# A recurrence kernel on one Trainium2 core: the loads of the next block are issued after another step of the chunk

## The reference, cut to what matters

```python
def step(carry, xs):
    W_in, W_out = carry
    q_t, k_t, v_t, lr_t = xs
    k_h = softmax(einsum('blhd,bDhd->blhD', k_t, W_in)) * lr_t[..., 1:]
    q_h = softmax(einsum('blhd,bDhd->blhD', q_t, W_in))
    qk = einsum('bqhD,bkhD->bhqk', q_h, k_h) * mask
    o_t = einsum('bqhD,bDhd->bqhd', q_h, W_out) + einsum('bhqk,bkhd->bqhd', qk, v_t)
    W_out = W_out + einsum('bnhD,bnhd->bDhd', k_h, v_t)
    for _ in range(2):
        g_out = -attn(W_in, k_t, v_t)
        g_in = -attn(W_out, v_t, k_t)
        W_in = W_in - lr_in * g_in
        W_out = W_out - lr_out * g_out
    return (W_in, W_out), o_t
```

## Time and profile before

| | us |
|---|---|
| median of 3 runs | 2461.43 |
| lowest and highest | 2460.49, 2465.33 |
| the profiled execution | 2457.74 |
| its span in the trace | 2456.0 |

### The profile page before, as it was taken

The page is one execution under the profiler, slowest core; times in us unless marked ns, Lnnn a source line. Parts: engine busy times, 40 slices in busy tenths (PEclk is TensorE's granted clock), DMA queues, the critical chain, the costliest instruction groups (busy, mean ns, idle before and its releaser), DMA issues.

```text
span 2456.0 us, 88067 instructions
## 1 busy us (share of the span) xinstructions
PE 2143.7 (87%) x32669; PEld 1375.5 (56%) x32669; DVE 1602.1 (65%) x3901; ACT 1558.3 (63%) x4121; POOL 1100.0 (45%) x1221
## 2 busy tenths in 40 slices
PE   7999996878888877885699999999999999999898
PEld 4455452555555555553366565665655756657566
DVE  6888885676776776773277474773746847557465
ACT  6788883676676676664365484564845748547474
POOL 1212223676776777776423344234433343233323
PEclk9999998898998898887799999999999999999999
DMA  6655557333334333411421312312123112220120
GB/s 199 179 154 161 175 152 186 69 67 82 77 68 88 79 69 75 87 32 37 134 69 44 91 22 76 78 45 74 38 76 77 45 52 60 74 72 11 33 52 18
DMA packets 387235, 201.37 MB, mean 82 GB/s; under 512 B 257376, under 2 KB 372704, under 8 KB 386800
## 3 DMA queue, kind: packets, MB, share of 16 engines
q1 hardware_dynamic: 386800, 195.65, 30.3%
HBM read 101.67 MB, written 69.27 MB: 70 GB/s over the span
## 4 chain that ended last, share of the span: by engine, by line
PE 44%; DVE 16%; issue 15%; ACT 14%; POOL 7%; SPq 2%; DMA 1%; ACTq 1%; DVEq 1%; POOLq 0%
PE psum L1050 11%; ACT arena L1569 8%; DVE arena L1861 6%; PE psum L1143 4%; PE psum L1102 3%; PE psum L906 3%; PE psum L1110 3%; PE psum L900 3%; ACT arena L1368 2%; POOL arena L1637 2%; PE psum L1216 2%; PE psum L893 2%; PE psum L914 2%; PE psum L1082 2%; PE psum L1179 2%
## 5 line engine op out<-in xcount | busy, mean ns | idle before, releaser
L1795 POOL TENSOR_TENSOR arena<-arena 128x400 f32<-128x400 f32 x256 | 218.3, 853 | 481.9 <-DVE arena L2223 481.9
L1368 ACT ACTIVATE arena<-psum,scan_sb 64x128 f32<-64x128 f32 x1152 | 307.7, 361 | 115.0 <-PE psum L974 107.0
L1569 ACT ACTIVATE arena<-psum,arena 128x100 f32<-128x100 f32 x1024 | 270.0, 367 | 6.4 <-DVE arena L2215 6.3
L1861 DVE SCALAR_TENSOR_TENSOR arena<-psum,taps_sb,arena 128x511 f32<-128x511 f32 (+2 forms) x288 | 212.5, 747 | 55.1 <-ACT arena L1268 48.4
L808 PE MATMUL psum<-arena,w_in_sb 128*128 128x512 f32 x512 | 230.1, 598 | 1.0 <-ACT arena L1261 1.0
L1611 POOL TENSOR_TENSOR arena<-arena 128x512 f32<-128x512 f32 x64 | 80.7, 1273 | 264.5 <-ACT arena L1294 264.5
L900 PE MATMUL psum<-arena 128*32 128x17 f32 x10240 | 127.3, 192 | 80.7 <-issue 60.0
L1940 DVE TENSOR_TENSOR arena<-psum,scan_sb 64x512 f32<-64x512 f32 x290 | 188.5, 673 | 3.3 <-PE psum L1006 2.9
L2215 DVE TENSOR_REDUCE arena<-psum 128x4 f32<-128x400 f32 x256 | 146.3, 573 | 58.5 <-PE psum L1166 48.1
L1561 ACT ACTIVATE arena<-psum 100x512 f32<-100x512 f32 x256 | 156.1, 610 | 42.8 <-PE psum L1179 36.6
L906 PE MATMUL psum<-arena,scan_sb 128*128 128x512 f32 (+1 forms) x328 | 172.3, 612 | 11.1 <-ACT psum L1413 4.5
(11 more groups left out here) (225 smaller groups left out, 4711.7 us busy)
## 6 DMA issues: line engine op xcount, KB each, us to landing
arena<-arena SPq DMA_DIRECT2D x144, 128.0 KB
arena<-x SPq DMA_DIRECT2D x32, 512.0 KB, 4.0
arena<-gates_d SPq DMA_DIRECT2D x112, 128.0 KB, 4.0
v_rows_d<-arena SPq DMA_DIRECT2D x64, 136.0 KB
k_rows_d<-arena SPq DMA_DIRECT2D x64, 136.0 KB
arena<-k_rows_d SPq DMA_DIRECT2D x128, 68.0 KB, 2.1
arena<-v_rows_d SPq DMA_DIRECT2D x128, 68.0 KB, 2.3
v_d<-arena SPq DMA_DIRECT2D x32, 256.0 KB, 4.5
```

The costliest lines, as they stand in the source:

```text
L1368: ins = act.activation(dst.rearrange("p (t x a) -> p t x a", x=PP, a=INNER)[upper, :, x], src.rearrange("p (t a) -> p t a", a=INNER)[upper ...
L1569: act.activation(c_soft[s][:, f % 2, u], sc, ACT.Exp, bias=c_max[s][:, u:u + 1]).then_inc(c_act.mark(f"exp{s}{f}u{u}"), 1)
L1795: pool.tensor_tensor(soft, soft, c_rec[s].unsqueeze(2).broadcast_to([P, 4, KEYS]), ALU.mult).then_inc(c_pool.mark(f"prob{s}{f}"), 1)
L1861: ins = dve.scalar_tensor_tensor(out=a_acc[:, t, j:TOK], in0=bank[2 + t][:, 0:TOK - j], scalar=taps_sb[:, t % KT, col:col + 1], in1=a_acc[ ...
```

## The change

In `feed`, SP's wait ahead of the block loads names another step of TensorE's semaphore. Nothing else differs: the same transfers, in the same order on SP, with the same sizes.

```diff
@@ -615,7 +615,7 @@
                     c = n * CPR + j
                     part = (j % CPB,)
                     if j < CPB or not last:
-                        sp.wait_ge(re_pe.sem, re_pe.at(c, "a0"))
+                        sp.wait_ge(re_pe.sem, re_pe.at(c, "p1v"))
                         hold(sp)
                         if j < CPB:
                             load_block(n * 2 + 1, 1, part)
```

## The result

The changed kernel takes 2484.4 us (median; 2477.4 to 2491.0) where the kernel before takes 2463.1 in the same session (2460.5 to 2472.9). The ratio is 1.0075, with a 95% interval of 1.0055 to 1.0095: some 18 us slower (the medians lie 21 us apart). The profiled execution took 2489.8 us, span 2488.0. It is one of the longest of the nine, and 32 us longer than the profiled execution of the kernel before, so what the two traces differ by is more than the change costs on average.

What follows compares the result with a forecast made beforehand. The prediction took latency along each chunk's chain in the recurrence as the bound, with no engine full. A gain of 5.0 us and a loss of 5.5 us summed to +0.5 us on 2461.4: 2462 us, range 2452 to 2474.

Steps and rivals of the forecast that it cites:

- the five crossings: TensorE crosses five instruction blocks a chunk: in p2v, about b0's 35th record, in pb0, in a1, before p1v.
- SP itself: SP's later wait and three issues, done by 723.2, would not hold up the row loads at 724.61: 0 us.
- row loads: Eight loads SP issues after p2v, needed at the next p1v: 0 us, 10 us in hand for landing.
- last part of a block: The block's fourth part, issued in its last chunk, needed at the next a0: 0 us, 9 us in hand.
- Gain at A: Crossing in p2v: packet freed from block traffic, shorter break, 0.18 us in 28 chunks, 5.0 us gained.
- Loss at B: Crossing about b0's 35th record: packet delayed under block traffic, 0.25 us in 22 chunks, 5.5 us lost.
- C: Crossing in pb0, after 22 records: nothing in the sum, named only as possibly falling within the new traffic.
- Clock: TensorE's granted clock, low a second time in seven chunks: 3.8 us either way, in the range, not the sum.
- no change: Whole kernel: within about 0.2% (4.9 us), the most a measurement can't tell from the old time; chance 0.42.
- Rival (2): b0: packet waits until block traffic ebbs, 0.7 us break in 28 chunks, +14.6 us, 2476; with mixtures, chance 0.28 for slower.
- The rule on the queues: DMA engines alternate queues packet by packet, so b0's packet would hardly wait, cost nothing, and the 5.0 us gain stay.
- rival (1): Only the gain in p2v: packets slip through full traffic, b0's 0.95 us covers the delay; 2456.4 us, chance 0.28.

Runs made afterwards that it cites:

- The shifts: Kernel before with 20, 43, 63, 87 or 107 extra matmul records once ahead of the recurrence: ratios 1.0486, 1.0795, 1.0472, 0.9926, 0.9928.
- the split load: Against the kernel before, q and k of the block load after a0 as before, v alone after p1v: 2461.3 us, 0.9982.
- the load behind p2v: Against the kernel before, the whole block loads wait for p2v instead of a0: 2478.2 us, 1.0046.
- 20 records: Kernel before with 20 more idle matmul records once ahead of the recurrence: 2587.5 us, 1.0486.
- 43 records: Kernel before with 43 more narrow matmul records once ahead of the recurrence: 2663.1 us, 1.0795.
- 87 records: Kernel before with 87 more narrow matmul records once ahead of the recurrence: 2445.7 us, 0.9926.
- early, late and split loads: Block loads after a1 of the chunk before (2460.4 us), after p1v (2484.4) or p2v (2478.2), or only v after p1v (2461.3).
- the shifted kernels: Kernel before with 87 or 107 extra matmul records; the changed wait on top gives 1.0037 against 0.9926, and 1.0100 against 0.9928.

## Why the prediction was wrong, point by point

- **What bounds the kernel, and the five crossings.** Right, but that the break in p2v is in 31 of 32 chunks and not in all. The shifts show that the breaks belong to the instruction stream; the changed kernel broke at the place named for B, the 34th record (named: about the 35th).
- **SP itself, row loads, last part of a block.** Right: 0 us. The row loads start behind p2v as before, and the split load shows no cost of the wait.
- **Gain at A.** Right in kind, a little less: 0.13 us a chunk, 3.6 us, for 0.18 and 5.0.
- **Loss at B: right in kind, too small.** Named 0.25 us in 22 chunks, 5.5 us. Measured 7.9 us in 14 breaks. The packet's delay was well forecast: 1.0 us on average, inside my 0.7 to 1.5. Two things were off. I took one time in hand, 0.95 us, for all chunks. The way from the break to b0's 35th record varies by 1.0 us between chunks; in the one shown above b0 starts after 3.72 us and not 4.29, so 0.4 us are in hand. And I counted the delay up to the packet's start only; where b0 breaks, it is 2.7 us on average from there to its use, and not 2.5.
- **C: the first step that failed.** I put it at nothing in the sum and named it only as something that might shift. It breaks 14 times where it broke once, 4.5 us more. Ten of the 14 are in chunks where B broke too; a late block B leaves less time for the next one.
- **Clock: the second step that failed, and the larger.** It was left out of the sum, as two chunks either way "with no sign that I can give". It fell in each kernel with the full load at p1v, by 0.006 to 0.0135 of its mean over the execution, and the estimate above puts it at 6 of the 18 us. With it the sum would have been outside "no change". It does not simply follow the breaks: the load behind p2v has fewer of them and a lower clock. What brings it down stays open.
- **Rival (2)**, 14.6 us slower, had the right side and nearly the size, by another way: it wanted 0.7 us in all 28 chunks, and half of them broke, for 0.56 us on average. That it came out near is in part luck, since C and the clock made up what B lacked. It also said that the packet waits until the burst has ebbed. The packet at 740.0 in the middle of it speaks against that.
- **The rule on the queues.** By the Trainium skill ("DMA: Bandwidth & Descriptors", Queues, rings and completion order) each DMA engine takes the queues in turn, packet by packet. The packet at 740.0 did go in between the others, which agrees with it; but it came 0.95 us late all the same, and that is enough for a break. So the rule's "B would cost nothing", on which rival (1) leaned, did not hold.

## What to carry to other kernels

Where one engine runs hundreds of short instructions in each step, look for idle time that no semaphore explains, at the same place in each step, and for the packets of the instruction queues between the bursts of data: a transfer that can move freely should be over before such a packet is due, or start behind it. Take the time in hand from several chunks at both levels of the clock, not from one. And before judging any change in such a kernel by tenths of a per cent, shift its instruction stream by some dozen instructions: here this alone is worth between -0.7 and +8%.

## What the runs showed of the hardware that I had not expected

- TensorE crosses a block of instructions every 127 to 128 matmul records with their weight loads. In the dense stretch from `sums` to khv a crossing is a break of 1.9 us on average. From one crossing to the use of the next block go 1.2 + 2.5 = 3.7 us when nothing is in the way; where the work between two crossings takes longer, as up to B in the kernel before (4.0 us at the least), there is no break. The Trainium skill ("Runtime: NRT & Kernel Launch", Instruction fetch mechanics) has blocks of 256 instructions, which agrees, and calls their cost mostly hidden, which doesn't: the breaks are 65 us of this kernel.
- The place of these crossings alone moves the time from 2446 to 2663 us. The breaks' own length is half of the loss with 20 records (67 of 123 us) and less than a third with 43 (59 of 201 us). The granted clock in the recurrence falls with them, from 0.91 (87 records) to 0.77 (20 records) and 0.71 (43 records) over its first 690 us.
- Where DVE's loop over rounds returns, the engine stands still for 2.3 to 3.4 us with nothing to wait for. It shows up to three times in a trace, in kernels with early, late and split loads alike.
- Open: what lowers the clock under late loads; why the load behind p2v costs 11 us with no more breaks than before; what makes up the 7 to 11 us that breaks and clock leave over when the change is put on the shifted kernels.
